# Eight groups of four generator calls in place of sixteen pairs

## What is computed

```
# second layer, its last part (per token)
x = x + f_alpha * ((silu(h @ gate_w.T) * (h @ hidden_w.T)) @ out_w.T + out_b)
# third layer: each batch has weights of its own
dWd = ((h_lang @ Wdd.T + bdd) * 0.1).reshape(B, BN, D)
dWu = ((h_lang @ Wdu.T + bdu) * 0.1).reshape(B, D, BN)
down = relu(einsum('bld,bnd->bln', x, Wd + dWd) + bd)
x = x + einsum('bln,bdn->bld', down, Wu + dWu) + bu
```

## Time and profile before

| | us |
|---|---|
| median of 3 runs | 749.59 (749.37 to 749.69) |
| the profiled execution, device time | 748.37 |
| its span, first to last instruction | 746.6 |
| PE busy / DVE busy / ACT busy / POOL busy in it | 730.2 / 518.1 / 363.4 / 419.5 |
| the 16 pairs of generator calls | between 421.4 and 662.4 of the span |

### The profile page before, as it was taken

One profiled execution on the slowest core, in us unless ns is written; L12 is line 12 of the kernel. 1 busy time (PEld: TensorE's weight loads), 2 busy tenths in 40 slices (PEclk: granted clock), 3 DMA queues, 4 the chain that ended last, 5 costly groups with the idle time before them and its releaser, 6 DMA issues.

```text
span 746.6 us, 18077 instructions
## 1 busy us (share of the span) xinstructions
PE 730.2 (98%) x6406; PEld 597.5 (80%) x6406; DVE 518.1 (69%) x805; ACT 363.4 (49%) x719; POOL 419.5 (56%) x408
## 2 busy tenths in 40 slices
PE   8999999999999899999999999999999999999996
PEld 6888888888888799999988777677677767778884
DVE  3977778777789988888985464646655565553467
ACT  4444444444447687888875323333333332322585
POOL 4756646655678888999987533424242423320244
PEclk9999999999999999999999999999999999999998
DMA  8955344444433010000004355476757777759953
GB/s 244 296 108 107 86 118 106 106 120 117 99 81 74 12 36 3 2 1 0 2 4 127 76 185 178 153 243 204 203 181 246 215 223 222 243 161 389 387 179 129
DMA packets 80810, 105.69 MB, mean 142 GB/s; under 512 B 39760, under 2 KB 53168, under 8 KB 80624
## 3 DMA queue, kind: packets, MB, share of 16 engines
q1 hardware_dynamic: 79600, 103.32, 46.9%
q10 hardware_dynamic: 1152, 1.59, 1.0%
HBM read 75.23 MB, written 21.26 MB: 129 GB/s over the span
## 4 chain that ended last, share of the span: by engine, by line
PE 90%; DVE 3%; POOL 3%; issue 2%; DMA 1%; ACT 1%; SPq 0%; DVEq 0%; POOLq 0%; ACTq 0%
PE banks L435 23%; PE banks L1202 22%; PE banks L1232 12%; PE banks L1048 5%; PE banks L1254 4%; PE banks L1125 4%; PE banks L452 4%; PE banks L1083 3%; PE banks L1166 3%; PE banks L1141 2%; PE banks L1863 2%; PE banks L1107 2%; PE banks L1833 2%; DMA early<-in_up_t 1%; PE banks L1855 1%
## 5 line engine op out<-in xcount | busy, mean ns | idle before, releaser
L1584 DVE TENSOR_TENSOR g<-banks,silu 128x512 f32<-128x512 f32 x64 | 44.1, 689 | 79.3 <-PE banks L1202 52.0
L1424 ACT ACTIVATE g_hi<-g 128x512 fp32r<-128x512 f32 x64 | 40.4, 631 | 97.8 <-DVE g L1584 96.7
L1588 DVE TENSOR_TENSOR g_lo<-g,g_hi 128x512 fp32r<-128x512 f32 x64 | 55.0, 859 | 47.5 <-ACT g_hi L1424 47.5
L1418 ACT ACTIVATE silu<-banks 128x512 f32<-128x512 f32 x64 | 38.2, 597 | 97.9 <-PE banks L1202 97.9
L435 PE MATMUL banks<-up_hi,xs_hi 128*128 128x512 f32 x256 | 81.9, 401 | 1.3 <-POOL xs_lo L364 0.8
L435 PE MATMUL banks<-up_lo,xs_hi 128*128 128x512 f32 x256 | 79.5, 391 | 0.5 <-DVE up_lo L694 0.5
L435 PE MATMUL banks<-up_hi,xs_lo 128*128 128x512 f32 x256 | 79.2, 391 | 0.0
L1202 PE MATMUL banks<-mlp_in_hi,w_hi 128*128 128x512 f32 x252 | 78.8, 394 | 0.0
L1202 PE MATMUL banks<-mlp_in_lo,w_hi 128*128 128x512 f32 x252 | 78.0, 391 | 0.0
L1202 PE MATMUL banks<-mlp_in_hi,w_lo 128*128 128x512 f32 x252 | 77.8, 390 | 0.0
L659 DVE SCALAR_TENSOR_TENSOR h<-banks,rstd,gelu 128x512 f32<-128x512 f32 x64 | 47.9, 748 | 35.4 <-ACT gelu L552 35.2
(11 more groups left out here) (224 smaller groups left out, 1806.3 us busy)
## 6 DMA issues: line engine op xcount, KB each, us to landing
gen_hyper<-in_gen_t SPq DMA_DIRECT2D x32, 512.0 KB, 4.5
gen_made<-base_w SPq DMA_DIRECT2D x64, 256.0 KB, 4.4
adapter_w<-gen_made SPq DMA_DIRECT2D x64, 256.0 KB, 4.4
tokens<-in_x_tok SPq DMA_DIRECT2D x32, 128.0 KB, 2.4
w_stage<-in_w_t SPq DMA_DIRECT2D x32, 128.0 KB, 2.4
tokens_again<-in_x_tok SPq DMA_DIRECT2D x32, 128.0 KB, 2.3
weight_slot<-adapter_w SPq DMA_DIRECT2D x4, 1024.0 KB, 8.9
x_sb<-in_x_t SPq DMA_DIRECT2D x7, 512.0 KB, 7.1
```

Of the source, the lines that this page charges most:

```text
L1418: nc.scalar.activation(silu[:, f % 2, :], chunk_bank(s, f, 0)[:, :], ACT.Silu).then_inc(S["silu_done"], 1)
L1424: nc.scalar.activation(gs[0][:, f % 2, :], g[:, f % 2, :], ACT.Copy).then_inc(S["g_hi_done"], 1)
L1584: nc.vector.tensor_tensor(g[:, f % 2, :], chunk_bank(s, f, 1)[:, :], silu[:, f % 2, :], ALU.mult).then_inc(S["g_done"], 1)
L1588: nc.vector.tensor_tensor(gs[1][:, f % 2, :], g[:, f % 2, :], gs[0][:, f % 2, :].bitcast(FP32), ALU.subtract).then_inc(S["g_ready"], 1)
```

## The change

The calls are grouped by four in place of two. `hyper` and `made` have four places each: calls 0 and 1 in the old two tiles, calls 2 and 3 in a new name `gen_more` and in the first 2048 columns of `early`. Both lie where the high and the low part of the attention weights are (their space is that of `w1_hi` and `w1_lo`), so SP now waits for the last product of attention (`o_ready`) before it loads the first group. The four calls still have two pairs of PSUM banks: calls 0 and 2 share banks 4 and 7, calls 1 and 3 banks 2 and 3. Before call 2 PE waits until DVE has copied call 0, before call 3 until call 1 is copied. DVE waits once, for all eight base transfers of a group; SP waits once for all eight stores. The eight groups stand at chunk 7 of tile 0, chunk 3 of tile 1, chunk 2 of tiles 2 and 4, chunk 1 of tiles 3 and 5, and chunks 1 and 7 of tile 6.

```
+        with ExitStack() as ch:
+            core["gen_more"] = sb("gen_more", [P, SLOT // 2], FP32, ch)
         w1_hi = sb("w1_hi", [P, W1], FP32R)
...
-        hyper, made = (ap[:].rearrange("p (k c n) -> p k c n", k=2, c=2) for ap in gen_space)
+        hyper, made = ([ap.rearrange("p (k c n) -> p k c n", k=2, c=2)[:, k] for ap in pair for k in range(2)]
+                       for pair in ((gen_space[0][:], core["gen_more"][:]), (gen_space[1][:], early[:, 0:SLOT // 2])))
...
+                return {1 if s.slot(1, 2) else 2: (s.turns, 3 if s.slot(1, 2) else 2)}
+            return {0: {7: (0, 0)}, 1: {3: (0, 1)}, 6: {1: (0, 6), 7: (0, 7)}, 7: {}}[t]
...
         def gen_ps(k):
-            return (bank[2], bank[3]) if k else (bank[4], bank[7])
+            return (bank[2], bank[3]) if k % 2 else (bank[4], bank[7])
...
                 if s.live(0):
-                    pair = s.at(0)
-                    for k in range(2):
-                        wait(sp, made_stored[k], 32 * pair)
+                    quad = s.at(0)
+                    wait(sp, made_stored, 128 * quad)
+                    for k in range(4):
                         for half in range(2):
...
+            sp.wait_ge(A["o_ready"], NA)
+            pipeline(sp, GEN_CALLS // 4, 1, 2, body)
...
-                for k in range(2):
-                    pe.wait_ge(hyper_loaded[k], 16 * pair + 16)
-                wait(pe, S["gen_copied"], 2 * pair)
+                pe.wait_ge(hyper_loaded, 64 * quad + 64)
+                wait(pe, S["gen_copied"], 4 * quad)
                 hold(pe, S["passed"])
-                for k in range(2):
+                for k in range(4):
+                    if k >= 2:
+                        pe.wait_ge(S["gen_copied"], 4 * quad + k - 1)
+                        hold(pe, S["passed"])
...
-                        for k in range(2):
-                            ve.wait_ge(S["gen_done"], 2 * pair + k + 1)
-                            ve.wait_ge(base_copied[k], 32 * pair + 32)
+                        ve.wait_ge(base_copied, 128 * quad + 128)
+                        for k in range(4):
+                            ve.wait_ge(S["gen_done"], 4 * quad + k + 1)
                             for chunk, ps in enumerate(gen_ps(k)):
```

More of the change, by code:

```diff
@@ L866, in output_ps, with quads, quad_number @@
             return bank[7 if s.last(4) else 4 if s.last(3) else 0]
-        def pairs(s):
+        def quads(s):
             t = s.at(1)
             if not isinstance(t, int):
[L872 to L877, removed]
+                return {1 if s.slot(1, 2) else 2: (s.turns, 3 if s.slot(1, 2) else 2)}
+            return {0: {7: (0, 0)}, 1: {3: (0, 1)}, 6: {1: (0, 6), 7: (0, 7)}, 7: {}}[t]
+        def quad_number(turn, first):
+            return 2 * turn + first
         def gen_ps(k):
-            return (bank[2], bank[3]) if k else (bank[4], bank[7])
+            return (bank[2], bank[3]) if k % 2 else (bank[4], bank[7])
         def chunk_bank(s, f, i):
@@ L898, in body @@
                 if s.live(0):
-                    pair = s.at(0)
-                    wait(sp, S["gen_done"], 2 * pair)
-                    for k in range(2):
-                        sp.dma_start(hyper[:, k].rearrange("p h n -> p (h n)"),
-                                     io["gen_t"][:, bass.ds((2 * pair + k) * 2 * GEN_N, 2 * GEN_N)]).then_inc(hyper_loaded[k], 16)
+                    quad = s.at(0)
+                    wait(sp, S["gen_done"], 4 * quad)
+                    for k in range(4):
+                        sp.dma_start(hyper[k].rearrange("p h n -> p (h n)"),
+                                     io["gen_t"][:, bass.ds((4 * quad + k) * 2 * GEN_N, 2 * GEN_N)]).then_inc(hyper_loaded, 16)
@@ L904, in body @@
                 if s.live(1):
[L905 to L907 removed]
+                    quad = s.at(1)
+                    for k in range(4):
+                        sp.wait_ge(S["gen_copied"], 4 * quad + k + 1)
                         for half in range(2):
[L909 to L910 removed]
+                            sp.dma_start(adapter_w[:, bass.ds(half * P // 2 * GEN_N + (4 * quad + k) * 2 * GEN_N, 2 * GEN_N)],
+                                         made[k][B * half:B * (half + 1)].rearrange("p q n -> p (q n)")).then_inc(made_stored, 16)
@@ L1236, in generate @@
             def generate(s, f):
-                if not s.live(1) or f not in pairs(s):
+                if not s.live(1) or f not in quads(s):
                     return
-                pair = pair_number(*pairs(s)[f])
-                if f == 6 and s.first_tile(1):
+                quad = quad_number(*quads(s)[f])
+                if s.first_tile(1):
                     pe.wait_ge(A["ot_done"], NA)
@@ L1254, in generate @@
                             last = nc.tensor.matmul(ps[B * half:B * (half + 1), :], scaled[rows, :],
-                                                    hyper[rows, k, half, :], start=True, stop=True)
+                                                    hyper[k][rows, half, :], start=True, stop=True)
                     last.then_inc(S["gen_done"], 1)
@@ L1628, in swiglu_body @@
                         scaled_mlp(s)
-                    if s.live(1) and f in pairs(s):
-                        pair = pair_number(*pairs(s)[f])
-                        for k in range(2):
-                            ve.wait_ge(S["gen_done"], 2 * pair + k + 1)
-                            ve.wait_ge(base_copied[k], 32 * pair + 32)
+                    if s.live(1) and f in quads(s):
+                        quad = quad_number(*quads(s)[f])
+                        ve.wait_ge(base_copied, 128 * quad + 128)
+                        for k in range(4):
+                            ve.wait_ge(S["gen_done"], 4 * quad + k + 1)
                             for chunk, ps in enumerate(gen_ps(k)):
-                                ins = nc.vector.tensor_tensor(made[:, k, chunk, :], made[:, k, chunk, :], ps[:, :], ALU.add)
+                                ins = nc.vector.tensor_tensor(made[k][:, chunk, :], made[k][:, chunk, :], ps[:, :], ALU.add)
                             ins.then_inc(S["gen_copied"], 1)
```

17 lines of the change are left out of this document (7 added, 10 removed).

## The result

The kernel with eight groups of four takes **778.45 us** in the median of four runs (777.69 to 786.92), the kernel before 749.48 in four runs beside it: a ratio of 1.0412, 95% interval 1.0387 to 1.0437. The change costs 29.0 us. The forecast was 770.1, in a range of 763 to 778: the direction and the largest term hold, the size does not.

A forecast was written before the change was run, and what follows sets the result against it. PE's program was taken as the bound. Terms of -2.0 + 15.9 + 1.8 + 3.1 + 1.7 = +20.5 us on the median of 749.59 gave 770.1 us, in a range of 763 to 778.

The forecast's parts named there:

- Bound: Over the SwiGLU and last stage PE's program sets the time; its waits were 1.7 us, so added waits are paid fully.
- Handovers: On PE, eight groups in place of sixteen pairs save 8 x 0.25 = 2.0 us.
- PE's two waits: Inside each group PE waits for DVE's copies before calls 2 and 3: 1.99 us a group, 15.9 us in all.
- Groups at chunk 1: In tiles 3, 5 and 6, DVE's adds start 0.6 us later behind `y_alpha`: 1.8 us in all.
- Base weights at group 1: Base transfers for tile 1's group land late, so DVE starts 3.1 us late and PE waits; bounds 0 and 8.
- The clock at group 1: A 4.8 us stop of PE there may lower the clock: 1.7 us, counted once, bounds 0 and 3.
- The rival by which it falls at every group: The clock falls at all eight groups, seven more losses of 1.7 us: 782 us, chance 0.06.
- Start and end: The generator's later first loads cost 0, with 3.9 us of cover; the last stage's weights come in step with PE, cost 0.

The follow-up runs named there:

- half groups: The changed kernel with two semaphores each for base transfers and stores, for calls 0 and 1 and for calls 2 and 3: 770.22 us, 1.0256.
- the other executions with plain groups: The changed kernel with split semaphores (770.22 us), with tiles 3 and 5's groups at chunk 2 (779.26), and with split semaphores plus ACT's row spread at chunk 7 (774.06).
- the first experiment: The kernel before the change, with SP waiting for the end of attention before it loads the first pair: 749.40 us, 0.9995.

## Why the prediction was right or wrong

*Bound.* Right: PE's program sets the time, and each stop put on it was paid.

*Handovers.* Right: three calls and one handover cost 3.08 us, by my prices 3.07.

*PE's two waits.* Right, the largest term: a group at 6.0 us, measured 6.03 to 6.08 where undisturbed. The split was a little off: stop 1.64 in place of 1.74, second stop 0.10 in place of 0.25, and some 0.3 more in the matmuls, for calls 2 and 3 took 2.19 us beside that stop and not 1.88. The bounds of this term were wrong by their own premises: they give 1.8 and 2.1 us a group, where I wrote 1.7 and 2.3.

*Groups at chunk 1.* The mechanism holds (`g_lo` beside POOL, `y_alpha` ahead), the size does not: late adds cost 3.7 us in place of 1.8. I took 0.6 for each group from the one tile that showed it. In the profiled execution one such group cost 2.4 and another nothing; where POOL's work lies decides, and that hangs on ACT's row. Two of the late places (tile 0 and the last group) aren't at chunk 1 at all.

*Base weights at group 1.* Right in kind and place, but this term was sized at half of what it cost, 6.3 us in place of 3.1, and is the largest part of the miss. The transfers were there 2.5 later than summed (1.4 for the stores, 1.0 for the base transfers' issue and landing), and DVE was ready for them 0.7 earlier, since PE's wait for `y_alpha` ahead was gone. The 238 GB/s that I summed with stands in no row; the earlier trace rows have 236 and 223, which makes up to 0.6 us of the difference. My upper bound of 8 held. The half groups show that the two waits for a whole bundle make it, SP's for eight stores and DVE's for eight base transfers: with both cut in two, nothing was late.

*The clock at group 1.* This step failed in its count. "Counted once" rested on one row: no fall behind a stop of 0.64 us. Between that and the 1.74 that I had just predicted for every group lay no row, and I said "hardly". The clock fell three times in both profiled executions of the changed kernel, for 4.3 us in all in the first, in which the price per fall, 1.25 to 1.64, is near my 1.7. The rival by which it falls at every group, with a chance of 0.06, was half true: three groups of eight, and the other executions with plain groups had three to five. The Trainium skill's rule of "TensorE: Matmul & The Clock Gate", section "A second HAM failure mode: psum-queue depth-cycling", by which such micro-idles make the clock swing, agrees with these rows, with 0.50 behind eight of the 29 stops under 2.6 us.

*Start and end.* Right: the late start costs nothing by the first experiment, and no transfer was late at the end.

*Not in the sum.* ACT's wait for its own 2 KB store. I looked at what the larger bursts do to SP's own transfers, and not at who else has one under way. It held ACT for 10.2 us in three places, PE for 1.2 in one, and made group 0's stop longer.

*The size of the miss.* The profiled execution was 29.7 us longer than before and not 20.5. Of these 9.2 us the base weights have 3.2, the clock 2.6, the late adds 1.9, and the three terms that the sum did not have 1.4 together.

*The range.* The three large misses lie on the same side. The clock is the link that I left out: a longer stop is paid as a stop, and behind it the clock is likelier to fall. The range had also left out bounds of its own: its high end took the dearer waits and 5 us at group 1, but neither the 2.1 more that I allowed for late adds nor the 1.3 more for the clock. With them it would have ended near 781, above the 778.45 measured.

## What to carry to other kernels

A wait put on the engine that sets the time costs its length, and on TensorE the slower matmuls behind it too, where the clock falls. So before calls are grouped, ask whether the group has as many banks as it has calls: three calls with three places beat four calls with two, though four save more handovers. Where transfers are bundled, keep the semaphores for parts of the bundle, since one wait for all of it puts the next transfer behind the last byte, and what uses the bundle behind its last part, and look whose small transfers share the engines with the burst.

## What the runs showed of the hardware beside this

- Behind stops of 1.64 to 2.57 us among 64x64 matmuls the clock fell at 8 groups of 29, and behind 2.68 us or more at all 11; a fall cost 1.1 to 1.7 us, once 1.9 and once 2.4. Filling the stops with unused matmuls took 5.5 to 5.8 us off a kernel.
- A store of 2 KB issued by ACT during SP's base transfers landed 7.4 us after its issue, where 1.4 is the median of the kernel before.
- Base weights, one DRAM row read for 64 partitions, moved at 234 to 236 GB/s with all DMA engines busy, where the loads and stores of a pair had 387 and 404.
- `g_lo` on DVE, 0.69 us at most while POOL was idle, took up to 2.73 us beside POOL's work on an input.
